# Constants in three loads, spare rows at the head, split tiles between the first eight pairs and the others

## The chip, the cores and the metric

The kernel runs on 1 core of one Trainium2 chip, in one launch. Its engines are TensorE (PE in the rows; PEld are its weight loads), VectorE (DVE), ScalarE (ACT), GpSimd (POOL), and SyncE (SP), which issues most of the DMAs. The metric is the device time of the launch in microseconds (us), the median of 3 runs. Lower is better.

## The reference: a delta-rule attention layer, then a mixture of 8 experts

Input `x` has 8 sequences of 512 tokens, width 256, in fp32: 4096 tokens. What is computed:

```python
# layer 1, per token, 4 heads, DK = 128, DV = 64
xn = layernorm(x)
q, k, v = xn @ Wq, xn @ Wk, xn @ Wv ; beta = sigmoid(xn @ Wb)
k = k * rsqrt(sum(k*k) + 1e-12) ; q = q * DK**-0.5
# delta rule, along the 512 tokens of each sequence
delta = (v_t - k_t^T S) * beta_t ; S = S + k_t delta^T ; o_t = q_t^T S
g = xn @ Wg
x = x + (o * rsqrt(mean(o*o) + 1e-5) * norm_w * g * sigmoid(g)) @ Wo
# layer 2, per token: top 2 of 8 experts, hidden 1024
xn2 = layernorm(x) ; probs = softmax(xn2 @ router_w.T)
x = x + sum over the two chosen experts e of probs_e * (gelu(xn2 @ w1[e].T) @ w2[e].T)
```

So each token has two rows of expert work: 8192 rows in all.

## The kernel before

**Stage 1, attention.** The 4096 tokens are 32 chunks of 128 (`T`), in a software pipeline: iteration i of one loop, written out in full, works on chunk i for some steps and on chunks i-1 to i-8 for others. Nothing schedules it: the order on each engine is that in which its block calls the step functions, and semaphores join the engines. One iteration takes some 14 us. `ln1_stats` (DVE), `ln1_scale` (POOL), `ln1` (ACT) and `xnT_make` (PE) normalise and transpose the tokens, `xnT_evac` (ACT) and `xnT_low` (DVE) cut the transposed block into a high and a low fp16 part, and `k_proj`, `q_proj`, `vg_proj` multiply it by weights that `weight_hi` (ACT) and `weight_lo` (DVE) have cut in the same way. `k_square`, `beta_exp` (ACT), `k_norm` (DVE), `kscale_` (POOL) and `k_prime` (DVE) scale k. Meanwhile the expert weights come from DRAM in pieces through one buffer `wst`: `split_hi` and `scale_piece` on ACT, `split_lo` on POOL, and SP's `piece(j)` waits until POOL has done piece j-1.

**The head.** One load brings all the constants, `fc`, 128 x 547 fp32: the identity (columns 0 to 127), two triangles (128 to 383) and small tables. One semaphore, `s_fc`, stands for all of it. DVE, POOL and PE each wait for it before their first instruction. DVE reads none of it in its first eight instructions; POOL reads the column of -0.5 for its power; PE reads the identity for its transposes. The order in the head is that of the lines ahead of each engine's loop.

**Routing.** Each chunk's normalised rows lie in `rowA`, and POOL's `scatter` writes each row twice with an indirect DMA into `routed_rows` in DRAM, where each expert has a region. Behind the regions lie 256 spare rows, which must hold zeros and a harmless output row. `spare_rows` makes them on POOL in iteration 4 of its loop: a memset of a part of `rowA`, one instruction for the row number, and four DMAs from POOL's own queue. ACT's `ln2` of chunk 4 waits for them.

**Stage 2, experts.** Tiles of up to 256 rows. A *pair* is 256 rows of one expert. A *split* tile holds two halves of 128 rows with an expert each (what is left of each expert's rows after its whole pairs). There are 28 pairs and 15 halves: 36 tiles, of which the last holds one half only. Before, tiles 0 to 27 are pairs and 28 to 35 are split. The first 8 pairs are chosen from the rows of the first five groups of four chunks, so that they can start ahead of the end of stage 1; the table of the others comes when all rows are routed (`other_counts`, `other_units`, `other_table`). On PE, step t transposes tile t+2 (`xT_make`), multiplies tile t+1 with w1 (`up`) and tile t with w2 (`down`). `up` of a pair is 48 products with 256 columns, of a split tile 96 with 128 columns, each half with its own weights. `down(t)` waits until DVE's `rows_out(t-1)` has read the sums of the tile before (`s_yrow`). ACT computes gelu (`hidden`), DVE the low part (`hidden_lo`). `rows_out` scales the sums by the gates, and POOL's `accumulate` adds them to `out` in DRAM, with one indirect DMA for each half of 128 rows (`s_acc` counts 16 for each).

The order of those DMAs matters. No token stands twice among the rows of one expert, but two halves of different experts can hold the same token. So a pair's two DMAs start one behind the other, after all of the earlier tiles have landed, while the second half of a split tile waits for the first one's landing too:

```python
for a in range(halves(i, q)):
    value = i * 128 + (32 * q + (16 * a if split(i, q) else 0))
    ...
        pool.wait_ge(s_acc, value)
```

Four tiles are a body. Body 0 is written out, 1 to 5 are a hardware loop, and 6 to 8 are written out. `rows_out(t)` on DVE waits until tile t-2 has landed, since it writes over that tile's buffer.

## Time and profile before

| | us |
|---|---|
| median of 3 runs | 923.59 (923.05 to 925.59) |
| the profiled execution's own time | 925.97 |
| its span, first to last instruction | 924.2 |
| PE busy | 850.5 (92% of the span) |
| DVE busy | 626.3 (68%) |
| ACT busy | 603.6 (65%) |
| POOL busy | 440.7 (48%) |

The span can be read as four parts: a head until about 50 us, in which the pipeline fills; the attention iterations until about 475; a drain until about 535, in which stage 1 ends and the first expert tiles start; and the expert tiles to the end, with a tail after PE's last product at 910.4 us. The page gives busy time of each engine over 40 slices; in most of them PE is at nine tenths.

### The profile page before, as it was taken

The numbers are of one execution on the slowest core, as the hardware profiler recorded it, in microseconds if no ns is written. First come the engines' busy times: TensorE is split into PE (matmuls) and PEld (weight loads), VectorE is DVE, ScalarE is ACT, GpSimd is POOL, SyncE is SP. The second block draws the span as 40 slices with busy tenths as digits, with TensorE's granted clock in tenths as the row PEclk, the third lists the DMA queues.
The fourth block names the chain that finished last, engine by engine and source line by source line (L and its number), as shares of the span: only waits on it lengthen the run. The fifth ranks groups of instructions, "written<-read, shape, count | busy, mean of one in ns | idle before, by whom it ended". The sixth has DMA issues, their size and how long they took to land. (4 is left out here: it accounts for less than half of the span.)

```text
span 924.2 us, 29858 instructions
## 1 busy us (share of the span) xinstructions
PE 850.5 (92%) x9998; PEld 673.3 (73%) x9999; DVE 626.3 (68%) x1832; ACT 603.6 (65%) x1645; POOL 440.7 (48%) x433
## 2 busy tenths in 40 slices
PE   2789999899999999999988889999999999999993
PEld 1468887788877877778876667777777777777771
DVE  4578898898988988889875765555455555544441
ACT  3478888888888888888766745554445555544440
POOL 2164555667677676776647543332222333332223
PEclk9899999999999999999986999999999999999997
DMA  6022222233233332323233243333222233322222
GB/s 211 2 59 84 86 65 76 83 94 103 86 103 89 98 103 73 105 84 98 83 105 87 82 104 58 55 47 50 46 46 46 46 56 53 49 46 44 40 25 29
DMA packets 50152, 66.96 MB, mean 72 GB/s; under 512 B 6448, under 2 KB 34352, under 8 KB 50032
## 3 DMA queue, kind: packets, MB, share of 16 engines
q1 hardware_dynamic: 36064, 46.20, 17.4%
q0 software_dynamic: 13424, 18.10, 11.6%
q8 instruction: 77, 1.26, 0.6%
q10 hardware_dynamic: 544, 1.05, 0.3%
q14 instruction: 43, 0.35, 0.1%
HBM read 41.84 MB, written 23.48 MB: 71 GB/s over the span
## 5 line engine op out<-in xcount | busy, mean ns | idle before, releaser
L768 ACT ACTIVATE inverse_levels<-ps 128x512 f16<-128x512 f32 (+1 forms) x324 | 169.8, 539 | 172.3 <-PE ps L1504 148.4
L750 POOL DMA_INDIRECT out<-inverse_levels,yidx x71 | 119.3, 1680 | 265.2 <-DVE inverse_levels L2195 188.0
L1131 PE MATMUL ps<-inverse_levels,w_hi 128*128 128x256 f16 (+1 forms) x1376 | 198.1, 255 | 0.4 <-issue 0.2
L1131 PE MATMUL ps<-inverse_levels,w_lo 128*128 128x256 f16 (+1 forms) x688 | 168.4, 255 | 0.0
L2168 DVE SCALAR_TENSOR_TENSOR KpAT<-kq_wvg,inverse_levels 128x512 f16<-128x512 f32 (+1 forms) x144 | 98.8, 688 | 91.4 <-ACT inverse_levels L768 91.3
L1131 PE MATMUL ps<-w_s,inverse_levels 128*128 x426 | 140.5, 379 | 4.7 <-DVE inverse_levels L2195 3.9
L1131 PEld LDWEIGHTS ps<-inverse_levels,w_hi 128*128 x1376 | 123.0, 98 | 13.9 <-issue 1.0
L1131 PE MATMUL ps<-w_s,KpAT 128*128 x426 | 116.1, 273 | 0.0
L1031 ACT ACTIVATE kq_wvg<-ps 128x512 f32<-128x512 f32 (+1 forms) x144 | 85.0, 590 | 41.6 <-PE ps L1131 38.1
L2191 DVE TENSOR_SCALAR inverse_levels<-ps,gate 128x256 f32<-128x256 f32 x71 | 31.1, 480 | 92.1 <-PE ps L1131 92.0
L768 ACT ACTIVATE inverse_levels<-kq_wvg 128x512 f16<-128x512 f32 (+1 forms) x144 | 89.8, 624 | 4.6
L1749 DVE CAST_PREDICATED inverse_levels<-mask_s,ps 128x256 f16<-128x256 int8 x192 | 82.2, 428 | 15.6 <-PE ps L1131 10.3
L597 POOL TENSOR_TENSOR kscale<-karg,fc 128x8 f32<-128x8 f32 x32 | 52.6, 1645 | 79.1 <-DVE karg L1679 79.1
L1131 PE MATMUL ps<-inverse_levels 128*128 128x64 f16 x1536 | 72.9, 194 | 8.6 <-DVE inverse_levels L1749 7.9
L1131 PE MATMUL ps<-wqk,inverse_levels 128*128 128x512 f16 (+1 forms) x263 | 77.9, 384 | 2.9 <-DVE wqk L1822 2.8
L1131 PEld LDWEIGHTS ps<-w_s,inverse_levels 128*128 128x128 f16 x426 | 41.7, 98 | 52.7 <-issue 6.3
L675 POOL DMA_INDIRECT routed_rows<-rowA,slot x64 | 66.5, 1039 | 18.9 <-issue 12.2
L1131 PEld LDWEIGHTS ps<-inverse_levels 128*128 128x128 f16 x1536 | 60.3, 99 | 19.9 <-DVE inverse_levels L1749 12.5
L1131 PE MATMUL ps<-inverse_levels,Lh 128*128 128x64 f16 x896 | 63.8, 194 | 10.4 <-ACT inverse_levels L768 6.9
L1131 PE MATMUL ps<-kq_wvg,inverse_levels 128*128 128x512 f16 (+1 forms) x263 | 73.0, 385 | 0.0
L1131 PEld LDWEIGHTS ps<-inverse_levels,w_lo 128*128 x688 | 67.5, 98 | 6.2
L1131 PEld LDWEIGHTS ps<-inverse_levels,Lh 128*128 128x128 f16 x896 | 46.7, 100 | 21.6 <-ACT inverse_levels L768 10.6
(237 smaller groups left out, 1921.8 us busy)
## 6 DMA issues: line engine op xcount, KB each, us to landing
wst<-w SPq DMA_DIRECT2D x58, 256.0 KB
inverse_levels<-eye SPq DMA_DIRECT2D x35, 256.0 KB, 2.7
x_s<-x SPq DMA_DIRECT2D x32, 128.0 KB, 2.6
out<-x_s SPq DMA_DIRECT2D x32, 128.0 KB, 1.7
x_s<-routed_rows SPq DMA_DIRECT2D x7, 260.0 KB, 2.8
Lh<-routed_rows SPq DMA_DIRECT2D x7, 260.0 KB, 2.8
Vp<-routed_rows SPq DMA_DIRECT2D x7, 260.0 KB
rowA<-routed_rows SPq DMA_DIRECT2D x7, 260.0 KB
```

Source lines behind the costliest of these rows:

```text
L597: return pool.tensor_tensor(dst, src, half_neg[:, 0:n], ALU.pow)
L675: pool.indirect_dma_start(out=routed, out_offset=bass.IndirectOffsetOnAxis(ap=slot[:, g % 2, k, c:c + 1], axis=0), in_=rowA[:, g % RG * C ...
L750: pool.indirect_dma_start(out=out, out_offset=bass.IndirectOffsetOnAxis(ap=yidx[:, q, a:a + 1], axis=0), in_=yrow[:, q % 2, a, :], in_offs ...
L768: return act.activation(dst, src, ACT.Copy, scale=scale)
L1031: act.activation(gelu, p_h[m].rearrange("p (m n) -> p m n", m=2)[:, :, 0:n], ACT.Gelu, scale=1.0 / W_SCALE).then_inc(s_gelu, 1)
L1131: return pe.matmul(dst, lhsT, rhs, start=start, stop=stop, **kw)
L1749: dve.copy_predicated(even(Y[:, lev - 1, :, :], lev), level_mask(lev, 0, H), packed(p_y[q], lev)).then_inc(s_ys[q], 1)
L2168: dve.scalar_tensor_tensor(hlo[:, q % 2, two, 0:n], hf[:, m, :].rearrange("p (m n) -> p m n", m=2)[:, :, 0:n], H_SCALE, hhi[:, q % 2, two, ...
L2191: step(dve.tensor_scalar(yrow[:, par, a, :], p_yo[a][:, 0, :], gate[:, par, a:a + 1], None, ALU.mult))
```

## The change

Three things, on SP, POOL, ACT, DVE and PE:

- The constants come in three loads with a semaphore each: the small tables first (columns 384 to 546), then the identity, and the triangles behind the second block of tokens. DVE waits for them after the second `ln1_stats` instead of ahead of its first instruction, POOL waits for the small tables alone, PE for the identity alone. ACT's and DVE's work on `wk` stands ahead of their work on the first transposed block.
- POOL fills two blocks of `rowA` with zeros as its first instruction and writes the row numbers behind the first `ln1_scale`; one DMA on SP's queue stores all 256 spare rows, behind the loads of the head. `spare_rows` goes.
- The eight split tiles become tiles 8 to 15, the other 20 pairs 16 to 35. The half tile is tile 15. It gets two loads of 64 rows each and a second, direct DMA on POOL that writes zeros to the unused rows of `out`, so that each tile counts 32. Bodies 0 to 3 are written out, 4 to 7 are the loop, and 8 is written out.

```diff
-            sp.dma_start(fc[:, 0:FCONST], fconst).then_inc(s_fc, 16)
+            sp.dma_start(fc[:, 3 * P:FCONST], fconst[:, 3 * P:FCONST]).then_inc(s_fc, 16)
+            sp.dma_start(ident, fconst[:, 0:P]).then_inc(s_ident, 16)
             sp.dma_start(wb_in[:, :, :], wb.rearrange("(k p) n -> p k n", p=P)).then_inc(s_wb, 16)
             sp.dma_start(wq_in, wq.rearrange("(k p) n -> p k n", p=P)).then_inc(s_wload[1], 16)
             load_x(1)
+            sp.dma_start(fc[:, P:3 * P], fconst[:, P:3 * P]).then_inc(s_tri, 16)
...
             init_inverse(2)
+            sp.wait_ge(s_spare, 2)
+            sp.dma_start(routed[SPARE:SPARE + PE_TOK, :].rearrange("(a p) n -> p a n", p=P), rowA[:, C:C + 2, :]).then_inc(s_spared, 16)
...
         def _(pool):
+            pool.memset(rowA[:, C:C + 2, :], 0.0).then_inc(s_spare, 1)
             pool.wait_ge(s_fc, 16)
...
-            def spare_rows():
-                pool.memset(rowA[:, C:2 * C, :], 0.0).then_inc(s_spare, 1)
-                pool.wait_ge(s_spare, 1)
-                pool.tensor_scalar(rowA[:, C:2 * C, D + 3], rowA[:, C:2 * C, D + 3], lane, float(B * N), ALU.add, ALU.add).then_inc(s_spare, 1)
-                pool.wait_ge(s_spare, 2)
-                for c in range(C):
-                    part = c % 2 * 64
-                    pool.dma_start(routed[SPARE + 64 * c:SPARE + 64 * (c + 1), :], rowA[part:part + 64, C + c, :]).then_inc(s_spared, 16)
...
             ln1_scale(0)
+            pool.wait_ge(s_spare, 1)
+            pool.tensor_scalar(rowA[:, C:C + 2, D + 3], rowA[:, C:C + 2, D + 3], lane, float(B * N), ALU.add, ALU.add).then_inc(s_spare, 1)
             ln1_scale(1)
             for i in range(T + 1):
-                if i == 4:
-                    spare_rows()
...
         def split(i, q):
-            return isinstance(i, int) and i * 4 + q >= PAIRS
+            return isinstance(i, int) and FIRST <= i * 4 + q < FIRST + SPLITS
 
         def halves(i, q):
-            return 1 if isinstance(i, int) and i * 4 + q == TILES - 1 else 2
-
-        def entry(i, q, a):
-            return i * 4 + q if not split(i, q) else PAIRS + 2 * (i * 4 + q - PAIRS) + a
+            return 1 if isinstance(i, int) and i * 4 + q == FIRST + SPLITS - 1 else 2
+
+        def entry(i, q, a=0):
+            if split(i, q):
+                return PAIRS + 2 * (i * 4 + q - FIRST) + a
+            return i * 4 + (q if isinstance(i, int) and i * 4 + q < FIRST else q - SPLITS)
...
                 pool.wait_ge(s_yrow, i * 4 + (q + 1))
-                for a in range(halves(i, q)):
+                for a in range(2):
                     value = i * 128 + (32 * q + (16 * a if split(i, q) else 0))
                     if not (isinstance(value, int) and value <= 0):
                         pool.wait_ge(s_acc, value)
+                    if a == 1 and halves(i, q) == 1:
+                        pool.dma_start(out[B * N:B * N + P, :], zrow[:, 0:D]).then_inc(s_acc, 16)
+                        continue
...
             evac(wb_s[:, 0, :, :], wb_in[:, :, :], A_SCALE)
+            weight_hi(0, wk_s[:, 0, :, :], wk_in)
             xnT_evac(0)
-            weight_hi(0, wk_s[:, 0, :, :], wk_in)
             weight_hi(1, wq_s[:, 0, :, :], wq_in)
...
-            dve.wait_ge(s_fc, 16)
             ln1_stats(0)
+            weight_lo(0, wk_s, wk_in).then_inc(s_wsl, 1)
             xnT_low(0)
             weight_lo(0, wb_s, wb_in[:, :, :])
-            weight_lo(0, wk_s, wk_in).then_inc(s_wsl, 1)
             ln1_stats(1)
+            dve.wait_ge(s_fc, 16)
+            dve.wait_ge(s_ident, 16)
+            dve.wait_ge(s_tri, 16)
```

The first instructions of DVE before. `st` and `mv` are the mean and variance of a block of tokens, `wqk` the k and q weights, `inverse_levels` the buffer that holds the transposed block:

```order
L1636 BN_STATS st<-x_s 128x6
L1639 BN_AGGR mv<-st 128x2
L1640 TENSOR_SCALAR mv<-mv 128x1
L1648 TENSOR_TENSOR inverse_levels<-ps,inverse_levels 128x256
L1822 SCALAR_TENSOR_TENSOR wb_s<-wb_in,wb_s 128x8
L1822 SCALAR_TENSOR_TENSOR wqk<-w_s,wqk 128x1024
L1636 BN_STATS st<-x_s 128x6
```

and now:

```order
L1650 BN_STATS st<-x_s 128x6
L1653 BN_AGGR mv<-st 128x2
L1654 TENSOR_SCALAR mv<-mv 128x1
L1836 SCALAR_TENSOR_TENSOR wqk<-w_s,wqk 128x1024
L1662 TENSOR_TENSOR inverse_levels<-ps,inverse_levels 128x256
L1836 SCALAR_TENSOR_TENSOR wb_s<-wb_in,wb_s 128x8
L1650 BN_STATS st<-x_s 128x6
```

The work on `wk` moved ahead of the two that need the transposed block and the small weight `wb`.

POOL around iteration 4 before. `rs` is the scale of a layernorm, `Ll` a low part that PE waits for, `w_lo_0` a piece of expert weights:

```order
L597 TENSOR_TENSOR kscale<-karg,fc 128x8
L660 TENSOR_TENSOR Ll<-nL,Lh 128x512
L680 MEMSET rowA 128x1040
L682 TENSOR_SCALAR rowA<-rowA,fc 128x4
L686 DMA routed_rows<-rowA 64x260 x4
L646 TENSOR_TENSOR w_lo_0<-wst,w_hi_0 128x512
L597 TENSOR_TENSOR rs<-mv,fc 128x1
```

and now:

```order
L612 TENSOR_TENSOR kscale<-karg,fc 128x8
L675 TENSOR_TENSOR Ll<-nL,Lh 128x512
L661 TENSOR_TENSOR w_lo_0<-wst,w_hi_0 128x512
L612 TENSOR_TENSOR rs<-mv,fc 128x1
L622 TENSOR_SCALAR rs<-mv,rs 128x1
```

Six instructions between the last step of one iteration and the first of the next are gone.

The end of POOL's program before, from the last step in the loop of bodies:

```order
L750 DMA out<-inverse_levels,yidx 4224x256 x2
L756 REGISTER_ALU
L756 COMPARE_AND_BRANCH
L750 DMA out<-inverse_levels,yidx 4224x256 x23
L76 UNCONDITIONAL_BRANCH
```

and now:

```order
L759 DMA out<-inverse_levels,yidx 4224x256 x2
L768 REGISTER_ALU
L768 COMPARE_AND_BRANCH
L759 DMA out<-inverse_levels,yidx 4224x256 x8
L76 UNCONDITIONAL_BRANCH
```

Of the 23 before, 8 were of pairs and 15 of halves; the 8 now are of the last four pairs.

## Rows read from the trace of the kernel before

**Rows 1.** Stretches: length, busy of PE, PEld, DVE, ACT, POOL, clock, DMA share, GB/s.
```profile
490.00:500.00 10.00, 8.21 (x85) 7.04 (x85) 5.22 (x21) 6.35 (x14) 6.21 (x7) 0.50 0.32 86
...
650.00:700.00 50.00, 50.00 (x391) 38.26 (x390) 26.67 (x59) 26.85 (x45) 16.69 (x10) 1.00 0.32 51
```

**Rows 2.** Timeline of the head: start, duration, engine, line, operation, idle before.
```profile
0.72 0.39 SPq L459 DMA_DIRECT2D x_s<-x  x1
...
1.64 0.43 SPq L494 DMA_DIRECT2D wb_in<-wb  x1
...
5.89 0.43 DVE L1636 BATCH_NORM_STATS2 st<-x_s 128x6 f32<-128x256 f32 x1 [5.89 <-DMA fc<-fconst]
...
7.86 0.60 ACT L776 ACTIVATE inverse_levels<-x_s,rs 128x256 f32<-128x256 f32 x1 [4.84 <-POOL rs L607]
...
9.58 1.99 ACT L768 ACTIVATE wqk<-w_s 128x1024 f16<-128x1024 f32 x2
...
10.74 1.22 DVE L1822 SCALAR_TENSOR_TENSOR wqk<-w_s,wqk 128x1024 f16<-128x1024 f32 x1
...
12.55 0.15 DVE L1640 TENSOR_SCALAR mv<-mv 128x1 f32<-128x1 f32 x1
...
20.11 1.66 POOL L597 TENSOR_TENSOR kscale<-karg,fc 128x8 f32<-128x8 f32 x1 [5.33 <-DVE karg L1679]
```

**Rows 3.** DMA issues until 30 us: KB each, us to landing; the last of x_s.
```profile
w_s<-wk ACTq DMA_DIRECT2D x1, 512.0 KB, 4.5
...
fc<-fconst SPq DMA_DIRECT2D x1, 273.5 KB, 4.7
...
wb_in<-wb SPq DMA_DIRECT2D x1, 4.0 KB, 5.8
...
DMA to landing us min/median/max: 2.8/5.7/6.0
```

**Rows 4.** Timeline around iteration 4: POOL, ACT and PE.
```profile
47.87 1.66 POOL L597 TENSOR_TENSOR kscale<-karg,fc 128x8 f32<-128x8 f32 x1 [9.12 <-DVE karg L1679]
...
53.23 2.44 POOL L686 DMA_DIRECT2D routed_rows<-rowA  x4 [0.33 <-POOL rowA L682]
...
63.76 1.65 POOL L597 TENSOR_TENSOR kscale<-karg,fc 128x8 f32<-128x8 f32 x1 [1.40 <-DVE karg L1679]
...
78.23 1.64 POOL L597 TENSOR_TENSOR kscale<-karg,fc 128x8 f32<-128x8 f32 x1 [2.08 <-DVE karg L1679]
...
57.97 0.60 ACT L776 ACTIVATE inverse_levels<-x_s,rs 128x256 f32<-128x256 f32 x1 [1.44 <-POOL rs L607]
...
60.66 0.29 PE L1131 MATMUL ps<-inverse_levels,Lh 128*128 128x64 f16 x4 [1.37 <-ACT inverse_levels L768]
```

**Rows 5.** Timeline of POOL: additions of pairs, then of halves, to the end.
```profile
760.42 1.56 POOL L750 DMA_INDIRECT out<-inverse_levels,yidx  x1 [7.14 <-DVE inverse_levels L2195]
762.28 1.87 POOL L750 DMA_INDIRECT out<-inverse_levels,yidx  x1 [0.30 <-issue]
771.38 1.55 POOL L750 DMA_INDIRECT out<-inverse_levels,yidx  x1 [7.22 <-DVE inverse_levels L2195]
...
827.71 1.55 POOL L750 DMA_INDIRECT out<-inverse_levels,yidx  x1 [9.11 <-DVE inverse_levels L2195]
...
900.45 1.55 POOL L750 DMA_INDIRECT out<-inverse_levels,yidx  x1 [5.83 <-DVE inverse_levels L2195]
...
919.09 1.55 POOL L750 DMA_INDIRECT out<-inverse_levels,yidx  x1 [3.00 <-issue]
```

**Rows 6.** Timeline of DVE and PE around the last two tiles.
```profile
898.75 0.88 DVE L2195 SCALAR_TENSOR_TENSOR inverse_levels<-ps,gate,inverse_levels 128x256 f32<-128x256 f32 x2
...
906.63 0.88 DVE L2195 SCALAR_TENSOR_TENSOR inverse_levels<-ps,gate,inverse_levels 128x256 f32<-128x256 f32 x2
...
907.64 0.39 PE L1131 MATMUL ps<-w_s,inverse_levels 128*128 x1 [2.04 <-DVE inverse_levels L2195]
...
910.14 0.27 PE L1131 MATMUL ps<-kq_wvg,KpAT 128*128 x1
```

More of the change, by code:

```diff
@@ L744, in accumulate @@
                 pool.wait_ge(s_yrow, i * 4 + (q + 1))
-                for a in range(halves(i, q)):
+                for a in range(2):
                     value = i * 128 + (32 * q + (16 * a if split(i, q) else 0))
@@ L1121, in _ @@
             expert_body(0)
-            with act.Fori(1, UNIFORM) as i:
+            for i in range(1, UNIFORM):
                 expert_body(i)
-            for i in range(UNIFORM, BODIES):
+            with act.Fori(UNIFORM, BODIES - 1) as i:
                 expert_body(i)
+            expert_body(BODIES - 1)
         @block.tensor
@@ L1493, in xT_make @@
             def xT_make(i, q):
-                if split(i, q):
-                    loads = 2 * (i * 4 + q - PAIRS) // 8 * 2 + halves(i, q)
-                    pe.wait_ge(s_xg[q % 4], 16 * (PAIRS // 4 + loads))
+                if isinstance(i, int):
+                    i, q = divmod(i * 4 + q, 4)
+                if isinstance(i, int) and i * 4 + q < FIRST + SPLITS:
+                    pe.wait_ge(s_xg[q], 16 * (i + 1) + 16 * max(0, i - FIRST // 4 + 1))
                 else:
-                    pe.wait_ge(s_xg[q % 4], i * 16 + 16 * (q // 4 + 1))
+                    pe.wait_ge(s_xg[q % 4], i * 16 + 16 * (q // 4 + 1 + SPLITS // 4))
                 if not (isinstance(i, int) and i * 4 + q < 1):
@@ L1608, in _ @@
             pe.wait_ge(s_tab, 2)
-            with pe.Fori(1, UNIFORM) as i:
+            for i in range(1, UNIFORM):
                 expert_body(i)
-            for i in range(UNIFORM, BODIES):
+            with pe.Fori(UNIFORM, BODIES - 1) as i:
                 expert_body(i)
+            expert_body(BODIES - 1)
         @block.vector
```

55 lines of the change are left out of this document (33 added, 22 removed).

## The prediction

> **What bounds the kernel now.** I read the busy time by stage first, then the timeline at the places that the change touches: the head, POOL around iteration 4, and the end. By stage: in the expert tiles PE is busy 50.00 of 50 us at a granted clock of 1.00, with DVE, ACT and POOL at about half or a third of that [rows 1]. There only a shorter PE program, or work taken out from in front of it or from behind it, moves the end. In the drain between the stages the granted clock is 0.50 (1.2 GHz) for whole stretches, and PE is busy 8.21 of 10 us [rows 1]. In the head one thing waits for the next: DVE's first instruction starts at 5.89 us, and the fence names the constants as its releaser, although it reads only tokens, which landed at 0.72 + 2.8 = 3.5 [rows 2, 3]. In iteration 4 ACT waits 1.44 us for POOL's scale, and PE 1.37 us for ACT [rows 4]. At the end PE is done at 910.14 + 0.27 = 910.4 [rows 6], but POOL issues its last addition at 919.09, 3.00 us after the end of the issue before it [rows 5], and the span ends at 924.2. So 13.8 us at the end are a chain of serial additions to DRAM, with no PE work in them. These three places are what the change can give back.
>
> **The head.** The chain before: statistics of block 0 from 5.89, POOL's scale, ACT's layernorm at 7.86 + 0.60 = 8.46, and only then wb, the transposed block, wk and wq on ACT, and wk on DVE at 10.74; the statistics of block 1 are done at 12.55 + 0.15 = 12.70, and from there the chain hangs together down to the scale of k at 20.11 [rows 2]. Now:
> - The tokens are there at 3.5, so the first link starts 2.4 us earlier, and the layernorm of block 0 ends at 8.46 - 2.37 = 6.1. POOL needs the small tables for that once DVE's three instructions are done, a little after 4. They are 163 of 547 columns; the whole load landed at about 5.9 while the tokens ahead of it landed at 3.5, which is 273.5 KB in 2.3 us [rows 2, 3]. At that rate 81.5 KB take 0.7 us: 4.2.
> - ACT converts wb first. It landed at 1.64 + 5.8 = 7.4 before [rows 2, 3]. Now 128 KB fewer lie ahead of it, 1.1 us at the same rate: 6.3. Issuing one more load ahead of it (0.43 us each [rows 2]) stays within that, as the queue is full of bytes and not of issues.
> - Then wk on ACT (half of 1.99) to about 7.6, on DVE (1.22) to 8.8 [rows 2], and behind it the low parts of the block and of wb, an estimate of 0.7 with gaps from the 1.22 of an operation four times as large, and the statistics of block 1, which end 12.70 - 11.96 = 0.7 behind the work on wk in the rows. That is 10.3 instead of 12.7, a gain of 2.4. wk itself landed at 0.7 + 4.5 = 5.2 [rows 3], so it is no bound. I take 2.2, since the triangles now come behind the second block of tokens and DVE needs them at about 10.
> - From below: if the loads stay as late as before and wb lands at 7.4 again, only the new order counts. wk is then done on ACT at 8.6 and on DVE at 9.9, and the statistics at 11.4: 1.3. From above: wb at 5.8, 2.9.
>
> A rule speaks against this part. The Trainium skill, DMA: Bandwidth & Descriptors, section Bandwidth, says to batch, since loads under 64 KB are bound by their descriptors, and the identity is just 64 KB. No row here shows a load of that kind alone; by this rule the small loads would land hardly sooner than the one large load, and the head would give its lower bound. The row of wb, 4 KB that took 5.8 us behind 273.5 KB [rows 3], agrees as far as that the bytes ahead of a load, more than its own, make it late, and that is why I stay near the upper value.
>
> **The spare rows.** POOL's memset, row number and four DMA issues go from iteration 4; the issues alone hold it 2.44 us [rows 4]. From scale of k to scale of k that iteration took 63.76 - 47.87 = 15.89, the next one 78.23 - 63.76 = 14.47 [rows 4]: 1.4 us too many, and PE's wait of 1.37 agrees. I take 1.4; at least 0 (a wait of another cause in its place), at most 2.4. What is added is hidden: the memset stands where POOL waits for the tables, the row number behind the first scale, when POOL would wait for the statistics of block 1, and the DMA on SP lies behind the loads of the head. It waits for POOL, and behind it on SP stand the loads of blocks 4 and 5 and of the first expert piece, none of which is used before iteration 3.
>
> **The split tiles in the middle.** Their extra cost moves with them. A pair takes PE 771.38 - 760.42 = 10.96 us, a split tile (900.45 - 827.71) / 6 = 12.12 [rows 5]; eight tiles at 1.2 more are paid at place 8 as at place 28. Tiles 8 to 15 fall into the stage where PE never waits [rows 1], and the second table is there long before. The added waits are on POOL: in a split tile two additions in series, each 1.55 to issue and 3.00 to land [rows 5], so 0.8 + 2 x 4.55 = 9.9 us of 12.1. The half tile's second, direct store has the same place. Behind the waiting POOL stand only further additions; DVE waits for the tile before last, a whole tile of slack. The loop and the written-out bodies show no gap in PE. I take 0, with 1 us either way.
>
> **The tail.** The last tile was half a tile behind a split one, now it is a pair behind a pair, so the additions of its two halves start without a wait in between, and nothing older is left to land. PE's sum of work is the same, its last `down` waits for the rows of the tile before in both (2.04 us [rows 6]), and so PE ends at 910.4 as before if nothing ahead moved. For a pair DVE is done at 906.63 + 0.88 = 907.51, and PE's product ended at 907.64 - 2.04 = 905.60: 1.9 us [rows 6]. POOL starts 900.45 - (898.75 + 0.88) = 0.8 later [rows 5, 6] and issues both in 1.55 + 0.30 + 1.87 = 3.7 [rows 5]. From the end of the last issue to the end of the span it is 924.2 - 919.09 - 1.55 = 3.6 [rows 5]. Together 910.4 + 1.9 + 0.8 + 3.7 + 3.6 = 920.4, so 3.8 less. What is late next: the additions of tile 34, ready one `down` of a pair and the wait earlier, twice the half tile's 2.8 us [rows 6], so at about 904.9. They are issued by 904.9 + 0.8 + 3.7 = 909.4 and landed by 912.4, before POOL wants to start at 913.1: 0.7 us of slack. Bounds: 3.0 if that slack is used up and more, 4.5 if the two issues overlap better.
>
> **The sum.** 2.2 + 1.4 + 0 + 3.8 = 7.4. Against the profiled execution, 925.97 with a span of 924.2, that gives 918.6. It stands 2.4 above the median of 923.59, so the median would be **916.2**. With all lower bounds (1.3 + 0 - 1 + 3.0 = 3.3) it is 920.3, with all upper ones (2.9 + 2.4 + 1 + 4.5 = 10.8) 912.8.
>
> **Rivals.**
> - *The drain meets the clock at another moment.* PE works at 0.50 of the clock through 490 to 500 [rows 1]. Everything up to there moves 3.6 us earlier, and a low stretch can cover more or less of the same products. Ten us at the low level with 8.21 busy hold 4.1 us that the high level would not take, so a stretch two thirds as long is worth some 3: 919.2, or 913.2. The spread of the three runs, 2.5 us, may already be this. The Trainium skill, TensorE: Matmul & The Clock Gate, Part 1, says that the activity window runs freely, so that the same kernel has a different number of slow matmuls from run to run. By that rule the 3 us fall by chance and belong to no part of the change.
> - *Only the tail pays.* The pipeline has a second limit behind the head (the weights' conversions, DVE's own order), and the early start is lost in the first iterations: the head gives 0 and iteration 4 gives 0. Against it: ACT and DVE wait in the head for each other and for POOL, not for DMAs that would stay where they are. 923.6 - 3.8 = 919.8.
> - *The serial additions stall the middle.* Slower than before. In a split tile the chain of 9.9 us has 2.2 us of room under 12.1. If an addition lands more than 1.1 us later in the middle than at the end, the chain is the tile's pace, DVE can't overwrite the rows and PE waits for DVE in `down`. With landings of 5.5 instead of 3.0 each of eight tiles costs 2 x 2.5 - 2.2 = 2.8, 22 us in all: 923.6 - 7.4 + 22 = 938. It outweighs the gains once a landing takes 1.6 us longer. Against it: in the kernel before, split tiles ran at this pace with the same chain, and the DMA share is 0.32 in the middle [rows 1].
> - *The half tile leaves a hole.* `up` and `down` of the half tile are 2.8 us each instead of 5.5, so ACT, DVE and POOL get less time there once; at most one wait like the 2.04 [rows 6]: 918.2.
>
> **How the numbers follow.** The forecast with its own range, 913.5 to 919: 0.66. The drain at another phase by more than that, upward: 0.12. Only the tail: 0.10. The half tile: 0.05, inside the range. The serial additions: 0.04. Something not seen, of either sign: 0.03. The range 912.5 to 920.3 leaves out the serial additions and the ends of the clock's case. What a measurement of this kernel can tell from no change is 0.3%, or 2.8 us: faster is below 920.8. Faster holds all but the serial additions, a part of the clock's and the tail's cases and of the unseen: 0.92; same 0.04; slower 0.04.
>
> **What would show it.** Head right: DVE's first statistics at about 3.5 instead of 5.89, the scale of k at about 17.9 instead of 20.11. Wrong if the first scale on POOL waits for the tables. Iteration 4 right: no wait of ACT for POOL near 54, the iteration at 14.5. Middle right: steps of 12.1 for tiles 8 to 14 and 10.9 for 16 to 35, no wait on PE. Wrong if PE waits for DVE there. Tail right: POOL's last two additions 0.30 apart, and some 10 us from PE's last product to the end instead of 13.8. The whole is wrong if the time is above 920.8, or if PE's last product stands less than 2 us or more than 6 us earlier.

## The result, and the profile after

The changed kernel takes 919.95 us (median of 10 runs, 915.98 to 923.75), the kernel before 925.48 beside it (10 runs, 923.05 to 930.65): ratio 0.9939, 95% interval 0.9919 to 0.9959. That is 5.5 us less where 7.4 were forecast, and the forecast of 916.2 lies 3.7 below the median. The range of 912.5 to 920.3 held, by 0.35 us.

The profiled execution of the changed kernel is the slowest of its ten, 923.75 with a span of 921.9. Its span is only 2.3 us below that of before (924.2). So this one trace is good for each local step, but not for the whole.

The head after, in the timeline of DVE, POOL and ACT (start, duration, engine, line, operation, idle before and what ended it):

```profile
3.35 0.43 DVE L1650 BATCH_NORM_STATS2 st<-x_s 128x6 f32<-128x256 f32 x1 [3.35 <-DMA x_s<-x]
...
5.68 0.58 POOL L612 TENSOR_TENSOR rs<-mv,fc 128x1 f32<-128x1 f32 x1 [4.44 <-DMA fc<-fconst]
...
6.67 0.60 ACT L787 ACTIVATE inverse_levels<-x_s,rs 128x256 f32<-128x256 f32 x1 [3.67 <-POOL rs L622]
7.23 0.21 ACT L779 ACTIVATE wb_s<-wb_in 128x8 f16<-128x8 f32 x1
7.35 1.04 ACT L779 ACTIVATE wqk<-w_s 128x1024 f16<-128x1024 f32 x1
8.42 1.23 DVE L1836 SCALAR_TENSOR_TENSOR wqk<-w_s,wqk 128x1024 f16<-128x1024 f32 x1 [4.25 <-ACT wqk L779]
...
18.33 1.66 POOL L612 TENSOR_TENSOR kscale<-karg,fc 128x8 f32<-128x8 f32 x1 [5.33 <-DVE karg L1693]
```

and the loads (KB each, us from issue to landing):

```profile
fc<-fconst SPq DMA_DIRECT2D x1, 81.5 KB, 4.4
fc<-fconst SPq DMA_DIRECT2D x1, 64.0 KB, 5.4
wb_in<-wb SPq DMA_DIRECT2D x1, 4.0 KB, 5.1
```

The statistics start at 3.35 instead of 5.89 [rows 2], but POOL then waits for the small tables until 5.68. They took 4.4 us, hardly less than the 4.7 of the whole load [rows 3]. `wb` landed at 2.12 + 5.1 = 7.2, where 6.3 was forecast, and ACT converts it at 7.23. The first scale of k is at 18.33 instead of 20.11 [rows 2].

Iteration 4, the timeline of POOL at its two ends:

```profile
46.81 1.66 POOL L612 TENSOR_TENSOR kscale<-karg,fc 128x8 f32<-128x8 f32 x1 [10.79 <-DVE karg L1693]
61.35 1.65 POOL L612 TENSOR_TENSOR kscale<-karg,fc 128x8 f32<-128x8 f32 x1 [1.40 <-DVE karg L1693]
```

It takes 61.35 - 46.81 = 14.54 us, before it took 15.89 [rows 4].

The split tiles, now in the middle: a stretch inside them and one of pairs (busy of PE, PEld, DVE, ACT, POOL; clock; DMA share; GB/s), and POOL's additions of two tiles' halves.

```profile
620.00:690.00 70.00, 69.86 (x753) 54.51 (x751) 34.46 (x87) 31.46 (x55) 19.15 (x12) 1.00 0.27 44
710.00:840.00 130.00, 130.00 (x1005) 98.71 (x1004) 67.34 (x156) 65.32 (x108) 40.89 (x24) 1.00 0.31 49
```

```profile
646.47 1.56 POOL L759 DMA_INDIRECT out<-inverse_levels,yidx  x1 [5.63 <-DVE inverse_levels L2211]
651.22 1.56 POOL L759 DMA_INDIRECT out<-inverse_levels,yidx  x1 [3.19 <-DMA out<-inverse_levels,yidx]
658.69 1.56 POOL L759 DMA_INDIRECT out<-inverse_levels,yidx  x1 [5.91 <-DVE inverse_levels L2211]
```

PE is as full as before. A split tile lasts 658.69 - 646.47 = 12.2 us, and the second half's addition waits 3.2 us for the first to land, as it did at the end before (3.00 [rows 5]).

The tail: PE's last `down` and the last products, then DVE and POOL.

```profile
904.86 0.39 PE L1143 MATMUL ps<-w_s,inverse_levels 128*128 x1 [2.04 <-DVE inverse_levels L2211]
...
906.31 0.63 PE L1143 MATMUL ps<-w_s,inverse_levels 128*128 x1
...
906.95 0.63 PE L1143 MATMUL ps<-w_s,inverse_levels 128*128 x1
...
911.64 0.27 PE L1143 MATMUL ps<-kq_wvg,KpAT 128*128 x1
```

```profile
912.02 0.88 DVE L2207 TENSOR_SCALAR inverse_levels<-ps,gate 128x256 f32<-128x256 f32 x2 [6.71 <-PE ps L1143]
```

```profile
914.63 1.55 POOL L759 DMA_INDIRECT out<-inverse_levels,yidx  x1 [5.68 <-DVE inverse_levels L2211]
916.49 1.55 POOL L759 DMA_INDIRECT out<-inverse_levels,yidx  x1 [0.31 <-issue]
```

From PE's last product (911.64 + 0.27 = 911.9) to the end of the span (921.9) it is 10.0 us instead of 13.8 [rows 5, 6], and the two additions are 0.31 apart. But PE ends 1.5 later than the 910.4 of before. Its last `down` took 911.91 - 904.86 = 7.05 us. In the 2 us before it PE is idle, in the next 4 the granted clock is near 0.50 (columns as above):

```profile
903.00:905.00 2.00, 0.14 (x1) 0.11 (x2) 1.93 (x7) 0.00 (x0) 0.00 (x0) 1.00 0.00 0
905.00:907.00 2.00, 2.00 (x9) 1.00 (x8) 0.27 (x2) 0.00 (x0) 1.46 (x1) 0.59 0.00 0
907.00:909.00 2.00, 2.00 (x8) 0.95 (x7) 0.00 (x0) 0.00 (x0) 1.64 (x2) 0.56 0.61 66
```

PE's products come 0.64 apart there (906.31 to 906.95) instead of 0.32.

**Where the gain of the head and of iteration 4 is.** The scale of k marks each iteration. It runs ahead of before by 1.8 us at the first, 2.7 at the fifth (behind iteration 4), 2.4 at the ninth, 1.1 at the tenth, 0.8 at the 28th, and at the 32nd it is 0.2 behind. The step of 1.3 is the iteration from 133.08 to 149.10 at a low clock, although PE is full in it:

```profile
144.00:148.00 4.00, 4.00 (x44) 3.54 (x43) 2.74 (x13) 2.60 (x12) 1.16 (x1) 0.57 0.27 68
```

The other large step, 1.0, is the iteration from 409.00 to 424.12. It is at full clock, but a piece of expert weights lands late and ACT stands still for it (waited for; us, times, longest):

```profile
ACT w_hi L779 <- DMA wst<-w: 1.0, 1, 1.0
...
PE ps L1143 <- ACT inverse_levels L779: 0.4, 1, 0.4
```

Before, that iteration took 423.97 - 409.81 = 14.16. Such waits come in both kernels, some at the same place (the iteration from 163.58 to 179.48, 164.24 to 180.15 before, has one of 1.8 us in both) and some not.

### The profile page after: what moved, and what is told of

It reads as the page before. It is cut to its first block, busy times and chain, and to the rows that moved or that the text cites. A ratio compares the mean times of both kernels' runs of the same rounds, so it can differ in the third digit from the quotient of the medians.

```text
span 921.9 us, 29756 instructions
## 1 busy us (share of the span) xinstructions
PE 854.7 (93%) x9998; PEld 675.8 (73%) x9999; DVE 625.9 (68%) x1832; ACT 603.7 (65%) x1645; POOL 443.1 (48%) x430
## 4 chain that ended last, share of the span: by engine, by line
PE 58%; POOL 6%; issue 5%; ACT 4%; DVE 4%; DMA 4%; SPq 1%; DVEq 0%; POOLq 0%; ACTq 0%
PE ps L1143 54%; DMA wst<-w 4%; PE ps L1517 2%; POOL kscale L612 1%; ACT inverse_levels L779 1%; POOL w_lo L661 1%; PE ps L1232 1%; POOL Ll L675 1%; POOL ors L612 1%; POOL w_s L661 1%; PE ps L1397 1%; POOL routed_rows L690 1%; DVE nL L1722 1%; DVE inverse_levels L1763 1%; POOL rs L612 1%
## 5 line engine op out<-in xcount | busy, mean ns | idle before, releaser
L612 POOL TENSOR_TENSOR kscale<-karg,fc 128x8 f32<-128x8 f32 x32 | 52.7, 1647 | 81.5 <-DVE karg L1693 81.5
```

The costliest lines, as they stand in the source:

```text
L612: return pool.tensor_tensor(dst, src, half_neg[:, 0:n], ALU.pow)
```

## The experiments

They ran on three chips, on which the kernel before takes 933.46 to 934.97 us (medians of 13 to 26 runs), 9 us more than in the pair above; the last section has what the traces show of that. I call them the other chips. Every ratio is to the kernel before on the same chip.

### The three parts, each alone

**Head alone**: the three loads, the semaphores and the order on ACT and DVE.

```diff
-            sp.dma_start(fc[:, 0:FCONST], fconst).then_inc(s_fc, 16)
+            sp.dma_start(fc[:, 3 * P:FCONST], fconst[:, 3 * P:FCONST]).then_inc(s_fc, 16)
+            sp.dma_start(ident, fconst[:, 0:P]).then_inc(s_ident, 16)
-            dve.wait_ge(s_fc, 16)
             ln1_stats(0)
+            weight_lo(0, wk_s, wk_in).then_inc(s_wsl, 1)
```

> The kernel before with the change of the head alone (three loads, the new order of wk on ACT and DVE, the later waits); spare rows and tiles as before. By my theory (each part pays for itself, and the clock's low stretches fall where they fall): the first scale of k at 18.3 instead of 20.1 us, and about 1.8 less in the median, 923.7 against 925.5; in one trace the gain can be gone by the drain if a low stretch of 3.4 us more lies on the way. By the rival that the pipeline behind the head has a second limit: 18.3 as well, but the gain shrinks in the first iterations in every trace and the median is that of before.

Measured: 932.43 us, ratio 0.9971 (0.9957 to 0.9985), 2.7 us less. POOL's scale of k:

```profile
17.98 1.66 POOL L601 TENSOR_TENSOR kscale<-karg,fc 128x8 f32<-128x8 f32 x1 [5.33 <-DVE karg L1683]
...
46.49 1.66 POOL L601 TENSOR_TENSOR kscale<-karg,fc 128x8 f32<-128x8 f32 x1 [10.80 <-DVE karg L1683]
62.34 1.65 POOL L601 TENSOR_TENSOR kscale<-karg,fc 128x8 f32<-128x8 f32 x1 [1.39 <-DVE karg L1683]
```

The first is at 17.98 (19.84 and 19.81 on the same chip in the two parts that leave the head as it was), and iteration 4 keeps its 62.34 - 46.49 = 15.85. So the head is real and independent of the spare rows. "Only the tail pays" falls.

**Spare rows alone.**

```diff
+            pool.memset(rowA[:, C:C + 2, :], 0.0).then_inc(s_spare, 1)
             pool.wait_ge(s_fc, 16)
...
-                if i == 4:
-                    spare_rows()
```

> The kernel before with the spare rows at the head alone. By my theory: iteration 4 (from the third to the fourth scale of k) takes 14.5 instead of 15.9 us, and the median is 1.4 lower. By the rival (another wait takes the place): 15.5 or more, and no difference in the median. The head must look as before, first scale of k at 20.1.

Measured: 932.36 us, ratio 0.9969 (0.995 to 0.9987), 2.9 us less. POOL:

```profile
19.84 1.66 POOL L600 TENSOR_TENSOR kscale<-karg,fc 128x8 f32<-128x8 f32 x1 [5.33 <-DVE karg L1682]
...
47.42 1.66 POOL L600 TENSOR_TENSOR kscale<-karg,fc 128x8 f32<-128x8 f32 x1 [9.13 <-DVE karg L1682]
61.65 1.65 POOL L600 TENSOR_TENSOR kscale<-karg,fc 128x8 f32<-128x8 f32 x1 [1.40 <-DVE karg L1682]
```

The iteration is down to 14.23 and the head stays where it was. The interval (1.2 to 4.7 us) holds the 1.4.

**Tile order alone.**

```diff
-            return isinstance(i, int) and i * 4 + q >= PAIRS
+            return isinstance(i, int) and FIRST <= i * 4 + q < FIRST + SPLITS
```

> The kernel before with the new order of tiles alone. By my theory: steps of 12.1 us for tiles 8 to 14, no wait of PE for DVE there, and 10.0 instead of 13.8 us from PE's last product to the end of the span, so 3.8 less in the median. In the last step PE waits 2.04 us; if a low stretch of the clock falls on the last products they take 7.0 instead of 5.2 us and 1.7 of the 3.8 are gone in that trace. By the rival that the split tiles cost more in the middle: PE's last product stands 1.5 us later at full clock as well, and the median gives 2.3 or less.

Measured: 929.25 us, ratio 0.994 (0.9919 to 0.9961), 5.6 us less; the 3.8 lie at the interval's low end (3.6 to 7.6). The tail of its trace:

```profile
912.78 0.39 PE L1145 MATMUL ps<-w_s,inverse_levels 128*128 x1 [2.04 <-DVE inverse_levels L2211]
...
917.88 0.27 PE L1145 MATMUL ps<-kq_wvg,KpAT 128*128 x1
```

The same wait of 2.04, but the last `down` takes 918.15 - 912.78 = 5.4 us, at full clock. From 918.15 to the end of the span, 928.1, it is 10.0. Its iteration 4 takes 17.1 us, with 3.4 us at the low clock in it, so a single trace can be off by more than a part is worth.

**The changed kernel again**, with no edit, beside the three.

> The changed kernel, unchanged, for a second trace. By my theory (the clock decides what is left of the gains): the first scale of k again at 18.3, the four blocks of the tail again 10.0 us, but the low stretches of the granted clock in other places or of another sum than the 37.5 us before the end of PE's work, and the time between 916 and 923 with them: about half a microsecond for each microsecond of low clock with PE busy. By the rival that the gain of the head is lost by the program's own order: the same loss of 2.7 us between iteration 4 and the drain in this trace too.

Measured: 927.89 us, ratio 0.9921 (0.9901 to 0.9942), 7.1 between the medians, 7.4 by the ratio. The first scale of k is at 18.00, and it is 9.9 us from PE's last product to the end. Against the only trace of the kernel before, which is from the first pair, the lead shrinks here too, from 4.2 us at the fifth scale of k to 0.95 at the 32nd; with the head filled it does not (5.5 and 5.8). So the rival, that the program's own order loses the gain, is neither shown nor excluded. A third time, on another chip ("the changed kernel a third time" below), it was 0.9943 (0.992 to 0.9965). The mean of the three ratios is 0.9934, which is 6.1 us.

The parts sum to 11.2 us, the whole gives 7.4 beside them. With intervals of 1.3, 1.7 and 2.0 on the parts and 1.9 on the whole the gap of 3.8 is at the edge of noise; against the 6.1 it is 5.1. What the traces offer for it: all three of the changed kernel have two low stretches that no part's trace has at those places, in the ninth iteration (1.5 us) and in the last `down` (1.65). I have one trace of each part, so that this is the difference is argued, not shown. The run with the wait ahead of the last `down` filled, below, has neither stretch in its trace, and its ratio of 0.9939 is no better: that speaks against it.

### The last tile by halves

The changed kernel, in which the last tile's `down`, rows and additions go half by half.

```diff
+                for a in range(2):
+                    for m in range(KH):
+                        ...
+                    last.then_inc(s_yops, 1)
```

> The changed kernel, with the last tile's `down`, its rows and its additions made half by half. The changed kernel goes from PE's last product to the end of the span in 10.0 us (two runs: 10.0 and 9.9), of which the two rows of both halves on DVE, POOL's first addition and the second one 1.87 us behind it are serial. Theory (that stretch is one chain from the last product, so a half that is finished earlier leaves earlier): the first half is done half a `down` (2.6 to 3.5 us) before the second, its addition is issued ahead of PE's end, and only one half's rows and one addition are left: 10.0 falls to about 7, ratio to the kernel before about 0.990 (the changed kernel 0.992 to 0.994). Rival (the end is set by POOL and the DRAM side of the additions, which cost 1.87 us one behind the other whenever they start): PE's end to span end stays at 9 to 10, ratio 0.993.

Measured: 926.69 us, ratio 0.9928 (0.9907 to 0.9948). POOL's additions of the last two tiles:

```profile
916.02 1.55 POOL L761 DMA_INDIRECT out<-inverse_levels,yidx  x1 [6.55 <-DVE inverse_levels L2237]
917.88 1.55 POOL L761 DMA_INDIRECT out<-inverse_levels,yidx  x1 [0.30 <-issue]
922.47 1.55 POOL L761 DMA_INDIRECT out<-inverse_levels,yidx  x1 [3.04 <-DMA out<-inverse_levels,yidx]
```

PE's last product ends at 922.39 and the span at 929.8: 7.4 us instead of 10.0. The first half's rows were done at 920.90, but its addition went out at 922.47, when the addition of the tile before had landed. So the first half meets the next limit, which is the serial landing: 922.47 - 917.88 = 4.6 us from issue to issue. The end hardly does in this trace: the second half's rows are done at 923.43, so its addition could not start much ahead of the 924.32 at which it does. The ratio alone could not have told any of that from the changed kernel.

### Does PE's idleness set the clock? Three places filled with unread products

**The head**, 16 products behind the transposes of block 1, where PE waits:

```diff
                 xnT_make(i)
+                if i == 1:
+                    for _ in range(16):
+                        mm(PS[3][:, :], wk_s[:, 0, 0, 0:P], wk_s[:, 0, 0, :])
```

> The changed kernel with 16 products of 512 columns put on PE behind the transposes of block 1, into a bank that nothing reads then; the results are not used. In the changed kernel PE has little to do there, and the granted clock is 0.50 (1.2 GHz) for 6.8 us from 17 on (10.2 in the other run). Theory A (the low clock at 17 to 27 is the answer to PE's idleness just before): the stretch goes or moves out of the head, and the time from the first to the fourth scale of k, 44 us, shrinks by 2 to 4 us; ratio about 0.990. Theory B (the low stretches are not caused by idleness at that place): the 6.8 us at 0.50 stay, within 3.4 us, and the time is that of the changed kernel, 0.993, or up to 1 us above it since 16 products at the low clock take 16 x 0.43 = 6.8 us of PE.

Measured: 925.3 us, ratio 0.9922 (0.9895 to 0.9948). Stretches of the changed kernel, then of this one:

```profile
16.00:18.00 2.00, 0.44 (x2) 0.20 (x2) 1.86 (x8) 0.76 (x4) 0.00 (x0) 0.97 0.34 122
18.00:20.00 2.00, 0.00 (x0) 0.00 (x0) 0.81 (x3) 0.00 (x0) 1.67 (x2) 0.50 0.00 0
20.00:22.00 2.00, 1.14 (x5) 1.00 (x6) 0.69 (x1) 0.02 (x1) 0.77 (x2) 0.50 0.00 0
```

```profile
16.00:18.00 2.00, 2.00 (x11) 1.05 (x12) 1.83 (x10) 0.34 (x1) 0.09 (x1) 1.00 0.17 64
18.00:20.00 2.00, 1.80 (x9) 0.60 (x7) 0.82 (x2) 0.00 (x0) 2.00 (x2) 1.00 0.00 0
20.00:22.00 2.00, 1.56 (x10) 0.97 (x10) 0.56 (x2) 0.60 (x1) 0.35 (x2) 1.00 0.00 0
```

The low stretch is gone: PE works at 2.4 GHz instead of 1.2 when the real work comes. From the first to the fourth scale of k it takes 40.65 us (17.91 to 58.56) instead of 43.0 (18.33 to 61.35), and 41.9 to 43.5 in the seven traces of this family with the head unfilled. Theory A holds for the clock and, with 1.2 to 2.9 us, for the chain; a later stretch of 3.4 us at the low clock, from 33.6 on, stays. The time alone shows no gain: 0.9922 lies among the three ratios of the changed kernel, 0.9921 to 0.9943.

**The wait in front of the last `down`**, 9 products:

```diff
+                    if isinstance(i, int) and i * 4 + q == TILES - 1:
+                        for _ in range(9):
+                            mm(PS[0][:, :], w2_s[:, 0, 0, 0:P], w2_s[:, 0, :, :].rearrange("p v n -> p (v n)"))
                     down(i, q)
```

> The changed kernel with 9 unread products of 512 columns put on PE in front of the last tile's `down`, where PE waits 2.04 us for DVE. In both runs of the changed kernel that `down` then took 7.05 us with the granted clock at 0.50 for 3.4 us, but 5.4 at full clock in the kernel with the tile order alone, which waits the same 2.04. Theory A (the wait sets the clock down): with the wait filled the last `down` takes 5.2 to 5.4 us, ratio about 0.991. Theory B (the dip comes for another reason, the wait is not it): 7.05 or 5.4 as it falls, the same as without, ratio 0.993.

Measured: 928.01 us, ratio 0.9939 (0.9918 to 0.9959). PE:

```profile
909.64 2.10 PE L1143 MATMUL ps<-w_s 128*128 128x512 f16 x9
911.84 0.39 PE L1143 MATMUL ps<-w_s,inverse_levels 128*128 x1
...
916.94 0.27 PE L1143 MATMUL ps<-kq_wvg,KpAT 128*128 x1
```

917.21 - 911.84 = 5.4 us, at full clock. Over all traces that have this pair at the end: with the wait unfilled, six of eight have the low stretch in the last `down` (7.0 us or nearly so), with the wait filled none of three. That points to the wait, but in two of the eight the same 2.04 us of idleness is followed by full clock, so it is not shown that the wait alone decides it. The whole time shows nothing of it.

**The drain**, pairs of products at seven places of each iteration behind the last block:

```diff
+            def keep_busy(i):
+                if i > T:
+                    done(pe, s_gs, T - 1)
+                    for _ in range(2):
+                        mm(PS[2][:, :], w1_hi[0][0][:, 0:P], w1_hi[0][0][:, 0:4 * P])
```

> The changed kernel with pairs of unread 512-column products put on PE at seven places of each iteration after the last block of the drain (from about 478 us on), where the trace has PE waiting for DVE and ACT. There the granted clock is at 0.50 for 20 to 27 us in all between 476 and 518 in every run. Theory A (the waits of the drain set the clock down): less than 10 us at 0.50 are left between 476 and 518, and the drain, 478 to 526, is 4 to 8 us shorter, ratio 0.985 to 0.989. Theory B (clock and idleness are not tied that closely, or the products themselves stand in the way of the chain): as much time at 0.50, and up to 3 us more of PE's time on the chain, ratio 0.993 to 0.997.

Measured: 927.1 us, ratio 0.9937 (0.9917 to 0.9957). Its stretches:

```profile
490.00:500.00 10.00, 8.20 (x98) 6.30 (x97) 5.03 (x16) 6.51 (x21) 7.49 (x8) 1.00 0.45 130
500.00:510.00 10.00, 7.21 (x52) 5.92 (x53) 5.85 (x16) 9.06 (x17) 7.84 (x8) 0.87 0.16 55
```

Before, the clock was 0.50 through 490 to 500 [rows 1], and in the three traces of the changed kernel the low level takes 20.5 to 27 us between 476 and 519. Here 3.4 are left. But from the last scale of k to the first of the last eight scatters it is 57.8 us (463.29 to 521.12), against 59.0 to 60.9 in the eight traces of this family with the drain unfilled (58.5 with the tile order alone). The ratio is that of the changed kernel. So theory A is right on the clock and wrong on the price: the drain hangs on ACT, DVE and POOL in turn, and my rival's 4.1 us for a low stretch of ten was too high.

### The small tables' landing, and all together

**POOL writes the -0.5 itself**, and ACT takes `wk` ahead of `wb`:

```diff
+            pool.memset(half_neg[:, :], -0.5).then_inc(s_half, 1)
             pool.memset(rowA[:, C:C + 2, :], 0.0).then_inc(s_spare, 1)
-            pool.wait_ge(s_fc, 16)
+            pool.wait_ge(s_half, 1)
```

> The changed kernel, with the -0.5 that POOL raises to written by POOL itself at the program's head instead of read from the small tables, and with wk converted ahead of wb on ACT. In the changed kernel POOL's first scale stands still until 5.68 us for the small tables, 4.4 us after their issue, where the statistics were ready at about 4.3. Theory (that landing is what kept the head's gain at 1.8 instead of 2.2 us in the profile): POOL's first scale starts at 4.3 to 4.5, ACT's layernorm at 5.3 to 5.5, and the first scale of k at 17.0 to 17.6 instead of 18.0 to 18.3; ratio better by up to 0.001. Rival (the weights land at 7.2 and later and set the head by themselves): the first scale of k stays at 17.9 to 18.3.

Measured: 927.49 us, ratio 0.9915 (0.9882 to 0.9948). POOL:

```profile
4.51 0.58 POOL L614 TENSOR_TENSOR rs<-mv,minus_half 128x1 f32<-128x1 f32 x1 [3.22 <-DVE mv L1657]
```

The scale starts at 4.51, and the first scale of k is at 17.06, the earliest so far. Against 18.17 in the changed kernel beside it that is 1.1 us. The run changes two things at once, but the traces tell which of them the head hung on. In the changed kernel beside it (the third trace, told next) POOL's scale starts at 4.99, and ACT, done with its layernorm at 6.57, then waits for `wb`:

```profile
4.99 0.58 POOL L612 TENSOR_TENSOR rs<-mv,fc 128x1 f32<-128x1 f32 x1 [3.74 <-DMA fc<-fconst]
...
7.08 0.21 ACT L779 ACTIVATE wb_s<-wb_in 128x8 f16<-128x8 f32 x1 [0.51 <-DMA wb_in<-wb]
```

Over the traces in which ACT takes `wb` first (us; the start of POOL's first scale stands for the landing of the small tables, the start of ACT's `wb` for that of `wb`):

| trace | POOL's first scale | ACT's `wb` | first scale of k | behind ACT's `wb` |
|---|---|---|---|---|
| changed kernel, first | 5.68 | 7.23 | 18.33 | 11.1 |
| second | 4.99 | 6.91 | 18.00 | 11.1 |
| third | 4.99 | 7.08 | 18.17 | 11.1 |
| head alone | 5.00 | 6.88 | 17.98 | 11.1 |
| last tile by halves | 5.05 | 7.02 | 18.11 | 11.1 |
| last wait filled | 4.95 | 7.45 | 18.54 | 11.1 |
| drain filled | 5.16 | 7.11 | 18.21 | 11.1 |
| head filled | 4.91 | 6.81 | 17.91 | 11.1 |

The scale of k follows `wb` to 0.02 us and not the tables: the trace with nearly the earliest tables has the latest scale of k. With `wk` ahead of `wb` this tie is gone: `wb` is converted at 7.21 there, and the scale of k stands 9.85 behind it. So by these rows the -0.5 alone would have made ACT wait longer for `wb` and gained next to nothing, and the order alone, with `wk` at 6.5 instead of 7.19, would have given an estimated 0.6 to 0.7 of the 1.1. Neither was run by itself. The ratio is not clear of that of the changed kernel.

**The changed kernel a third time**, for comparison with the runs of this group.

> The changed kernel once more, beside the others of this call, as what they are to be compared with. By the two measurements so far its ratio is 0.9939 and 0.9921: expected 0.992 to 0.994, a first scale of k at 18.0 to 18.3, a low stretch of 6.8 to 10.2 us from 16 or 17 on, and 9.9 to 10.0 us from PE's last product to the end. If the dip in the last `down` comes from the wait in front of it, it is there again (7.05 us); if not, 5.4 us is as likely.

Measured: 929.56 us, ratio 0.9943 (0.992 to 0.9965), the first scale of k at 18.17, the low stretch in the last `down` again.

**Four additions together**: the edits of own -0.5, head filled, last wait filled and last tile by halves, as shown above.

> The changed kernel with four additions together: POOL's own -0.5 and wk first, 16 unread products behind the transposes of block 1, 9 unread products in front of the last `down`, and the last tile's `down`, rows and additions half by half. Singly they gave in the profiles: 0.5 us forecast for the first, -3.5 us between the first and the fourth scale of k for the second, a last `down` at full clock for the third (1.6 us), and 10.0 to 7.4 us behind PE's last product for the last. Theory (they add up, since they lie one behind the other on the path): 7 to 8 us below the changed kernel, ratio to before 0.984 to 0.988. Rival (what is gained early is given back later, as the head's 2.7 us were within the attention stage of the first profile): only the two at the end count, ratio 0.989 to 0.991.

Measured: 921.05 us, ratio 0.9849 (0.9819 to 0.9879), 8.5 us below the changed kernel. The theory holds, the rival falls. The fourth scale of k is at 55.59 instead of 61.23 (5.6 us), and this time the lead is kept (5.8 at the 32nd). At the end two gains fell together. From the first addition of the tile before the last to the end it is 16.3 us in the changed kernel (912.33 to 928.6), 14.7 with the wait filled, 13.8 with the halves, and 13.7 with both:

```profile
907.16 1.55 POOL L764 DMA_INDIRECT out<-inverse_levels,yidx  x1 [6.54 <-DVE inverse_levels L2246]
909.02 1.55 POOL L764 DMA_INDIRECT out<-inverse_levels,yidx  x1 [0.30 <-issue]
913.55 1.55 POOL L764 DMA_INDIRECT out<-inverse_levels,yidx  x1 [2.98 <-DVE inverse_levels L2237]
```

The page names DVE for the 2.98, but the issue is 4.53 behind the one before, the same as with the halves alone, where it named the landing. The second half's rows are ready at 912.89 here, 2.5 us ahead of its addition at 915.40, where one step from rows to addition takes 0.8. So the serial additions are the last bound, worth some 1.7 us in this trace.

**The drain filled as well**, the same with `keep_busy`.

> As the one with four additions, and the pairs of unread products at seven places of the drain's iterations too, which alone took the time at 0.50 between 476 and 518 us from 20 to 27 down to 3.4 us, but the stretch from the last scale of k to the first scatters of the last two by only 1.2 to 2.0 us. Theory (the drain is set by chains over DVE, ACT and POOL, so the clock there is worth those 1 to 2 us and no more): 1 to 2 us below the kernel with four additions, ratio 0.982 to 0.987. Rival (the unread products stand in the way of the chain as often as the clock helps): the same as without, within 0.001.

Measured: 918.96 us, ratio 0.9838 (0.9811 to 0.9865), the best of all: 15.7 us below the kernel before, 10.6 below the changed one. It is 2.1 below the version without; the intervals overlap, so the extra is likely but not shown by the times. In its trace the drain takes 56.0 us, against 59.1 in the version without.

## Why the prediction was right, point by point

- **Sign and size.** 5.5 us beside the first trace, 6.1 over three measurements, 7.4 forecast (a ratio of 0.9920, at the edge of the first interval). Each of the three places gives back time for the reason that I gave, and each part is faster than before by itself. That the sum stays inside the range is in part luck: terms that I did not have went against it, and single traces differ by as much as the whole gain.
- **The signs that I had named.** Two of them say "wrong". The first scale on POOL does wait for the tables, until 5.68. And PE's last product should have stood 2 to 6 us earlier, but in the first pair of traces it stands 1.5 later. The changed kernel's trace there is the slowest of ten. The lead of 2.7 us behind iteration 4 was gone by the 32nd scale of k, ahead of the drain. On the other chips the 32nd scale of k stands at 465.75 and 465.05 in the changed kernel, and between 463.29 and 469.44 in three more traces of the same program up to there; with the tile order alone it is at 468.12. So the 3.6 us of the two early parts are seen in the times of the parts, and locally, but not as a lead that each trace keeps.
- **Head, 2.2.** 1.8 in the first trace. On the other chips 18.00, 18.17 and 17.98 stand against 19.81 and 19.84 with the old head, 1.6 to 1.9; in the time of the head alone it is 2.7 (1.4 to 4.0). The step that failed is the landing of `wb`: I put it at 6.3, 1.1 us sooner since 128 KB fewer lie ahead of it, and wrote that the one more issue stays within that. It landed at 7.2 (2.12 + 5.1) in the first trace and at 6.9 and 7.0 in the others. It took 0.7 us less from issue to landing (5.1 instead of 5.8 [rows 3]), but was issued 0.48 later (2.12 instead of 1.64 [rows 2]). The table above shows that the head hung on it in every trace. The small tables, put at 4.2 by the rate of bytes, were late too, about 5.6 in the first trace and 4.9 in the two others, but `wb` came later still, so that cost nothing that shows. Behind `wb` the chain to the statistics of block 1 was shorter than my estimate, 3.6 us (7.21 to 10.79) instead of 4.0, which made good a part of it. What the head gained came from the start no longer waiting for all the constants and from the new order on ACT and DVE. The rule of the Trainium skill that I weighed (DMA: Bandwidth & Descriptors, section Bandwidth: transfers under 64 KB are dominated by their descriptors) pointed the right way: by it my lower bound of 1.3, with `wb` at 7.4, was the closer case for the landing. Its price is not shown here, as no run has such a load alone: 81.5 KB took 4.4 us, 64 KB 5.4, 4 KB 5.1.
- **Iteration 4, 1.4.** 1.35 in the first trace. The head alone left it at 15.85, the move of the spare rows alone made it 14.23, and in the three traces of the changed kernel it is 14.54, 14.20 and 14.74. ACT's wait for POOL's scale is gone, as forecast.
- **Middle, 0.** The rows of the last tile but one are ready at 904.72, and I had put them at 904.9 by moving the tiles at equal cost. PE waits in the split tiles only once, 0.73 us as they begin, as before (0.66), and POOL waits for a landing mostly 3.2 us instead of 3.0, at most 3.8 there (670.71 to 676.09 from issue to issue): the rival "the serial additions stall the middle" falls, and "the half tile leaves a hole" too.
- **Tail, 3.8.** 13.8 to 10.0, and 9.9 to 10.0 in all eight traces that end on this pair with its halves together: as forecast. Inside the sum two terms were off by 0.3 in opposite directions, the two issues (3.4 instead of 3.7) and the way from the last issue to the end (3.9 instead of 3.6). What I had missed lies in front of it. I wrote that PE ends where it ended before "if nothing ahead moved", and it ended 1.5 later, since the last `down`, now of a pair and again behind 2.04 us of idleness, ran at half the clock for part of its length. Before, only the half tile's 2.8 us stood there, at full clock. I had read the 2.04 as equal in both.
- **The clock as a rival, 0.12.** Its place was wrong. I put it in the drain, where the low level takes 23.9 us before and 20.5 in the changed kernel's first trace, and filling the drain took only 1.2 to 3.1 us off it for some 20 us at the low level. It struck where PE is the bound: the last `down` (1.65) and the ninth iteration (1.5). In the ninth iteration the stretch came in three of three traces of the changed kernel, but not in that with the last wait filled, which is the same program up to there. In the head it came at 16 to 22 us in all eleven traces where PE was left idle and in none of the three where it was filled. The rule of the Trainium skill that I named (TensorE: Matmul & The Clock Gate, Part 1, that the number of slow matmuls differs from run to run by itself) fits the first and not the second.

In one line: the terms that the forecast got wrong are the landing of `wb`, 0.9 us late for 0.4 us of the head, and the clock in the last `down`, 1.65 us that it did not have. 7.4 less these two is 5.4, near the 5.5 that was measured. That match proves nothing: it takes terms of single traces from a difference of medians, the times of the run with that wait filled show no gain of 1.65, and the loss of the early lead, the largest in the first pair, is not in it.

## What to carry to other kernels

A wait ahead of a full PE stage can cost twice, by its length and by the clock behind it: here 2.04 us, and 1.65 more in six of eight traces. When a change puts a longer piece of PE work behind a wait, price that piece at the low clock too, and try unread products in the wait. In a stage that hangs on other engines the low clock was cheap, however long it looks in the profile: some 20 us of it were worth 1.2 to 3.1. When several loads move ahead, ask which one the chain waits for last: here it was 4 KB of `wb`, which landed only 0.3 us sooner in the first pair for all the bytes taken out ahead of it, and work that did not need it was better put in front.

## What the hardware showed beside

- **Seven to nine us at the start of the expert tiles on some chips.** Timeline of PE in the changed kernel, second time:

```profile
532.28 0.27 PE L1143 MATMUL ps<-inverse_levels,w_hi 128*128 128x256 f16 x1 [1.15 <-issue]
```

  Three to six gaps of 0.7 us or more for which no releaser is found stand there in the traces from the other chips, none in the first pair (which has one of 1.9 us, put down to DVE). POOL's last addition of the first tile and its first of the second are 13.5 us apart in this trace (537.3 to 550.9) and 4.6 in the first. All traces from the other chips also have 6.8 to 10.2 us at the low clock there, which the first pair has not. From the first addition to the first one of the third tile the other chips need 7.1 to 9.4 us more, most of the 9 us by which they are slower. What PE waits for there the profile does not say, and it was not tried.
- **A low clock with PE full.** A stretch of 3.4 us at 0.50 at this place, between 142 and 157 us, came in seven of the ten traces of the changed kernel and its variants, in the ninth iteration or, in the two runs with several additions together, in the tenth, and in none of the kernel before and the three parts. In the first trace PE is busy 3.00 of the 4 us ahead of it; in the trace with the last wait filled it is 3.00 too, and the clock stays at 1.00. Its cause is open.
- **The pace of additions into DRAM**: mostly 1.86 us from issue to issue where nothing is waited for, and mostly 4.3 to 5.1 where the first must land, with single ones up to 6.3 in the middle.
